# Cross attention on one core: head 3 scaled on VectorE, and V's last low-weight rows as a pair of 64-row matmuls

## The chip, the cores and the metric

One core of a Trainium2 chip. The metric is the device time of one execution in microseconds, the median of several.

## The reference

For each of 8 sequences, x is 256 x 256 and the context 256 x 192, all fp32; 16 heads of 64:

```python
h = layernorm(x) * gamma + beta
Q = (h @ Wq).reshape(B, 256, 16, 64)
K = (context @ Wk).reshape(B, 256, 16, 64)
V = (context @ Wv).reshape(B, 256, 16, 64)
attn = softmax(einsum("bihd,bjhd->bhij", Q, K)) * 64 ** -0.5
vals = einsum("bhij,bjhd->bihd", attn, V).reshape(B, 256, 1024)
out = x + vals @ Wo + bo
```

The scale stands behind the softmax, so no part of it can be moved into Q.

## The kernel before, in words

Products are made in fp32r, and each operand is split into a high part (the rounded value) and a low part (what the rounding left). A product is then high x high, high x low and low x high. ScalarE makes the high parts, VectorE or GpSimd the low parts. Scores are of these products; the probabilities and V stay whole.

The work is cut into 32 steps of four heads (two pairs a = 0, 1), four steps for a sequence. Each engine has its own list, written out by hand in a function `step(u)`, and runs through it in order; semaphores tie the lists together. TensorE's step u is: scores of step u; the first products of the next step's K (`keys_rest`); V x P of step u - 1 (`mix`); K and Q for step u + 1 (`keys`, `queries`); the output product of step u - 1 (`output`); in some steps the transposes of the next context (u = 4, 8, ...) or of the next x (u = 5, 9, ...); V (`values(u + 1)`, each a quarter of a sequence's V); and the transposes of step u's probabilities (`turn`), a first half for heads 0 and 1 and a second for heads 2 and 3. A step without a context or an x to turn is called ordinary below.

The softmax of step u: VectorE takes the maximum of each head's scores (`maximum`, L647), ScalarE the exponentials and their sums (`probabilities`, L457), VectorE the reciprocal of the sums (`inverse`, L654), and GpSimd scales the four heads, two instructions each (L369). ScalarE and VectorE copy the transposed probabilities out of PSUM (L541, L737). Between the heads the lists hold the high and low parts of the mix (L484, L696) and of the next K and Q (`keys_hi`, L467, and `keys_lo`, L660), which also free two PSUM banks: `values` writes its first half where the first pair's K and Q were, its second half where the second's were, and waits for `qk_lo_ready` each time.

V: the context has 192 columns, held as three K tiles of `c_t`: tile 0 the high part of the first 128, tile 2 their low part, and tile 1 both parts of the last 64, low part in the lower 64 partitions and high part in the upper. The weights' last 64 rows stand twice in tile 1 of `wv_hi` and `wv_lo`. `c_rest` holds the high part of the last 64 once more in the lower partitions; before the change only `keys_rest` uses it, for a pair of 64-row matmuls on the two row halves.

x: two buffers. SyncE loads sequence b into the buffer of b - 2 once GpSimd has normalised x (`x_norm`) and added the output bias to it (`x_bias`, L339). VectorE takes its statistics (`statistics`: two bn_stats L582, two bn_aggr L587, L590), GpSimd the power -0.5 (`deviation`, L324) and the normalisation (`norm`, L332; sequences 0 and 1 on VectorE, L596). For sequence b from 2 on the statistics belong to step 4b - 5. Weights arrive in 25 pieces; their low parts are made by VectorE (pieces 0, 4, 5, 8, 9, 13, 20, 21) or GpSimd (L318) in the first steps.

Of the kernel before, what the change touches and what calls it, by code (L numbers as in the profile page):

```python
# [6 lines left out]
def cross_attention_block(nc, x, ctx_in, w_q, w_k, w_v, w_o, b_o, gamma, beta, out):  # L7
# [10 lines left out]
    P = 128  # L18
# [49 lines left out]
    with ExitStack() as ctx:  # L68
# [60 lines left out]
        def qk_banks(u):  # L129

            return ring[u % 3]
# [60 lines left out]
        scaled = sem("scaled")  # L192
# [110 lines left out]
        def _(pool):  # L303
# [51 lines left out]
            def step(u, turns):  # L355
                if u == 1:
                    weight_lo(14)
                b = 1 if u == 1 else of_seq(u, TURN_C, 2)
                if b is not None:
                    deviation(b)  # L360
                    if b >= 2:
                        norm(b)
                if u == PER_SEQ:
                    weight_lo(23)
                if 0 <= u < STEPS:
                    for e in range(HEADS):
                        pool.wait_ge(inv_ready, HEADS * u + e + 1)
                        for r in range(RT):
                            last = nc.gpsimd.tensor_scalar(prob[:, e, r, :], prob[:, e, r, :],  # L369
                                                           inv[:, e, r:r + 1], SCALE,  # L370
                                                           ALU.mult, ALU.mult)
                        last.then_inc(scaled, 1)
                        if e == 1 and u == 2:
                            weight_lo(19)
                for n in {0: (10, 11, 12), 1: (15, 16, 17, 18)}.get(u, ()):
                    weight_lo(n)
                b = of_seq(u, SPLIT_H, 1)
                if b is not None:
                    hidden_lo(b)
                if u == 2:  # L380
                    weight_lo(22)

                    pool.wait_ge(bo_in, 16)
                    bias(0)

                b = 1 if u == PER_SEQ else b if u > PER_SEQ else None
                if b is not None:
                    if b >= 2:

                        pool.wait_ge(y_ready, b - 1)  # L390

                    pool.wait_ge(x_norm_ready, b + 1)
                    bias(b)
# [5 lines left out]
        def _(act):  # L399
# [42 lines left out]
            def step(u):  # L442
# [48 lines left out]
                if u == 2:  # L491
                    weight_hi(20)
                    weight_hi(21)
                    keys_hi(1)
                probabilities(3)
                if u != 2:
                    keys_hi(1)
# [69 lines left out]
        def _(dve):  # L567
# [10 lines left out]
            def statistics(b):  # L578
                k = b % 2
                dve.wait_ge(x_loaded[k], 16 * (b // 2 + 1))  # L580
                for r in range(RT):
                    last = nc.vector.bn_stats(bn[:, r, :], x_in[:, k, r, :])  # L582
                last.then_inc(stats_done, 1)
                dve.wait_ge(stats_done, b + 1)
                nc.vector.memset(var_eps[:, :], 0.0)
                for r in range(RT):
                    last = nc.vector.bn_aggr(mean_var[:, r, :], bn[:, r, :])  # L587
                last.then_inc(aggr_done, 1)
                dve.wait_ge(aggr_done, b + 1)
                nc.vector.tensor_scalar(var_eps[:, :], mean_var[:, :, 1], EPS, None, ALU.add)\  # L590
                    .then_inc(var_ready, 1)

# [34 lines left out]
            def step(u):  # L627
# [27 lines left out]

                def keys_lo(a):
# [17 lines left out]
                inverse(1)  # L674
                b = of_seq(u, PUT)
# [26 lines left out]
                if u == -1:  # L702
                    weight_lo(4)
                keys_lo(0)
                if u == -1:
                    weight_lo(5)
                if u != 2:
                    inverse(3)
# [6 lines left out]
                if u == 0:  # L715
                    statistics(1)
                if u == 1:
                    norm(1)
# [4 lines left out]
                if u == 2:  # L723
                    inverse(3)
# [3 lines left out]
                b = of_seq(u, STATS, 2)  # L728
                if b is not None:
                    statistics(b)  # L730
                if 0 <= u < STEPS:
# [8 lines left out]
                    if u == 0:  # L740
                        weight_lo(13)
# [5 lines left out]
        def _(pe):  # L747
# [189 lines left out]
            def turn(u):  # L937

                for a in range(BATCH):
                    pe.wait_ge(scaled, HEADS * u + 2 * a + 2)  # L940
# [9 lines left out]
            def values(n):  # L950


                g, j = divmod(n, RT)
# [6 lines left out]
                for a, ps in enumerate(((mix_ps, o_ps, mix_ps)[n],) if n <= RT else qk_banks(n)):  # L960
                    columns = PIECE if n <= RT else V_HALF
                    if n > RT:

                        pe.wait_ge(qk_lo_ready, BATCH * n + a + 1)
                    for m, (w, i, k) in enumerate(passes):
                        if m == CT and j == 0 and g in FOR_V:
                            low_ready(pe, FOR_V[g])
                        last = nc.tensor.matmul(ps[:, 0:columns], c_t[:, b % 2, k, rows],  # L968
                                                w[:, i, first:first + columns],
                                                start=m == 0, stop=m == len(passes) - 1,  # L970
                                                skip_group_check=True)
                    first += columns
# [81 lines left out]
```

## Time and profile before

| | |
|---|---|
| median of 3 runs | 335.07 us (335.03 to 335.29) |
| the profiled execution | 335.13 us, its span 333.3 |
| TensorE matmul | 323.3 us, 97% of the span |
| ScalarE | 254.8 us, 76% |
| VectorE | 234.6 us, 70% |
| GpSimd | 178.3 us, 53% |
| granted TensorE clock | full in all 40 slices |

Matmuls overlap in the records: one of 256 columns is recorded with 0.28 us, though the next starts 0.11 behind it. So TensorE's busy share says that it always has something in flight, not how much of its peak it reaches; the distance between starts is what counts. Times in the text are microseconds from the start of the span.

### The profile page before, as it was taken

Reading aid. Unit: us, or ns where it says so; the run is one execution under the profiler, and the core shown is the slowest. Engines: PE = TensorE matmul, PEld = TensorE weight load, DVE = VectorE, ACT = ScalarE, POOL = GpSimd, SP = SyncE. Lnnn points to the kernel's source line nnn. Section 1 sums busy time; section 2 is a strip of 40 time slices with the busy share of each in tenths; the row PEclk is TensorE's granted clock in tenths of the full one; section 3 lists DMA queues with packets and bytes.
Section 4 is the critical chain, followed back from the end, with each engine's and each line's share of the span. In section 5 each row is a group of like instructions: output and inputs, shape, how many; then the busy total and the mean of one; then the engine's idle time right before and its main releaser. Section 6 shows DMA issues by size and latency. Waiting matters only on the chain.

```text
span 333.3 us, 9654 instructions
## 1 busy us (share of the span) xinstructions
PE 323.3 (97%) x3773; PEld 284.3 (85%) x3773; DVE 234.6 (70%) x523; ACT 254.8 (76%) x799; POOL 178.3 (53%) x332
## 2 busy tenths in 40 slices
PE   5999999999999999999999999999999999999986
PEld 4868788899888899888889988889988888998864
DVE  5888667766778677676776677776677867556754
ACT  4899897777778766888667868777777876676772
POOL 4596778437473367543673456722757336344430
PEclk9999999999999999999999999999999999999999
DMA  6960010020000200020000200002000100000000
GB/s 181 266 185 3 1 41 18 2 89 2 0 2 31 60 3 0 2 89 2 3 4 0 89 2 2 0 3 89 2 2 1 33 3 3 2 0 33 2 3 31
DMA packets 10764, 10.70 MB, mean 32 GB/s; under 512 B 960, under 2 KB 10176, under 8 KB 10720
## 3 DMA queue, kind: packets, MB, share of 16 engines
q1 hardware_dynamic: 10192, 9.64, 9.6%
q8 instruction: 30, 0.49, 0.6%
q10 hardware_dynamic: 416, 0.33, 0.3%
q0 software_dynamic: 112, 0.13, 0.1%
q14 instruction: 14, 0.11, 0.1%
HBM read 8.00 MB, written 2.10 MB: 30 GB/s over the span
## 4 chain that ended last, share of the span: by engine, by line
PE 86%; ACT 6%; DVE 4%; POOL 2%; DMA 1%; issue 1%; DVEq 0%; ACTq 0%
PE mix_ps L823 16%; PE o_ps L914 12%; PE ring_ps L794 12%; PE ring_ps L889 12%; PE ring_ps L968 11%; PE ring_ps L944 10%; PE ring_ps L847 9%; ACT prob L457 3%; DMA x_in<-in_x_dram 1%; PE ring_ps L867 1%; POOL prob L369 1%; PE mix_ps L760 1%; PE mix_ps L768 1%; ACT qk_hi L467 1%; DVE prob_t L737 1%
## 5 line engine op out<-in xcount | busy, mean ns | idle before, releaser
L369 POOL TENSOR_SCALAR prob<-prob,inv 128x256 f32<-128x256 f32 x256 | 120.4, 486 | 129.2 <-DVE inv L654 129.1
L457 ACT ACTIVATE prob<-ring_ps,neg_max 128x256 f32<-128x256 f32 x256 | 119.3, 481 | 21.7 <-DVE neg_max L647 21.6
L647 DVE TENSOR_REDUCE neg_max<-ring_ps 128x2 f32<-128x512 f32 x128 | 81.4, 679 | 0.8 <-PE ring_ps L794 0.8
L737 DVE COPY prob_t<-ring_ps 128x512 f32<-128x512 f32 x64 | 41.4, 686 | 37.0 <-PE ring_ps L944 37.0
L823 PE MATMUL mix_ps<-prob_t,v_sb 128*64 128x256 f32 x504 | 61.5, 385 | 0.2 <-DVE prob_t L737 0.2
L660 DVE TENSOR_TENSOR qk_lo<-ring_ps,qk_hi 128x512 fp32r<-128x512 f32 x64 | 44.2, 690 | 17.7 <-ACT qk_hi L467 17.7
L457 ACT ACTIVATION_READ_ACCUMULATOR prob<-ring_ps,neg_max 128x1 f32 x256 | 54.4, 212 | 0.0
L823 PEld LDWEIGHTS mix_ps<-prob_t,v_sb 128*64 128x64 f32 x504 | 33.4, 136 | 18.1 <-issue 0.3
L527 ACT ACTIVATE v_sb<-ring_ps 128x256 f32<-128x256 f32 x58 | 19.2, 383 | 30.1 <-PE ring_ps L968 29.6
L467 ACT ACTIVATE qk_hi<-ring_ps 128x512 fp32r<-128x512 f32 x64 | 39.6, 619 | 1.2 <-PE ring_ps L889 1.2
L944 PE MATMUL ring_ps<-ident,prob 64*128 64x64 f32 x1024 | 39.3, 226 | 0.3 <-POOL prob L369 0.3
L794 PE MATMUL ring_ps<-qk_hi 64*128 64x256 f32 x256 | 39.1, 301 | 0.4 <-DVE qk_lo L660 0.3
L944 PEld LDWEIGHTS ring_ps<-ident,prob 64*128 64x128 f32 x1024 | 34.5, 139 | 5.1 <-POOL prob L369 1.0
L541 ACT ACTIVATE prob_t<-ring_ps 128x512 f32<-128x512 f32 x64 | 35.2, 599 | 3.3 <-PE ring_ps L944 2.1
L847 PEld LDWEIGHTS ring_ps<-c_t,w_hi 128*128 128x128 f32 x192 | 26.4, 188 | 11.9 <-issue 11.5
L794 PE MATMUL ring_ps<-qk_lo,qk_hi 64*128 64x256 f32 x256 | 36.1, 277 | 0.0
L914 PE MATMUL o_ps<-wo_hi,mix_hi 128*128 128x256 f32 x124 | 34.5, 278 | 1.7 <-DVE mix_lo L696 1.4
L794 PE MATMUL ring_ps<-qk_hi,qk_lo 64*128 64x256 f32 x256 | 36.1, 277 | 0.0
L847 PE MATMUL ring_ps<-c_t,w_hi 128*128 128x256 f32 x192 | 35.4, 294 | 0.1
L914 PE MATMUL o_ps<-wo_lo,mix_hi 128*128 128x256 f32 x124 | 34.4, 277 | 0.0
L914 PE MATMUL o_ps<-wo_hi,mix_lo 128*128 128x256 f32 x124 | 34.3, 276 | 0.0
L654 DVE RECIPROCAL inv<-sums 128x2 f32<-128x2 f32 x128 | 21.0, 164 | 17.9 <-ACT prob L457 16.6
(110 smaller groups left out, 638.2 us busy)
## 6 DMA issues: line engine op xcount, KB each, us to landing
x_in<-in_x_dram SPq DMA_DIRECT2D x8, 256.0 KB, 2.9
out_dram<-y_sb SPq DMA_DIRECT2D x7, 256.0 KB, 2.2
c_in<-in_ctx_dram SPq DMA_DIRECT2D x7, 192.0 KB, 2.8
w_raw<-in_L_xattn_Wq_dram SPq DMA_DIRECT2D x8, 128.0 KB, 3.1
w_raw<-in_L_xattn_Wo_dram SPq DMA_DIRECT2D x4, 256.0 KB, 4.0
w_raw<-in_L_xattn_Wk_dram SPq DMA_DIRECT2D x4, 128.0 KB, 3.7
w_raw<-in_L_xattn_Wk_dram SPq DMA_DIRECT2D x8, 64.0 KB, 3.5
w_raw<-in_L_xattn_Wv_dram SPq DMA_DIRECT2D x2, 256.0 KB, 4.7
```

The costliest lines, as they stand in the source:

```text
L369: last = nc.gpsimd.tensor_scalar(prob[:, e, r, :], prob[:, e, r, :], inv[:, e, r:r + 1], SCALE, ALU.mult, ALU.mult)
L457: last = nc.scalar.activation(prob[:, e, r, :], score_bank(u, e)[:, r * ROWS:(r + 1) * ROWS], ACT.Exp, bias=neg_max[:, e, r:r + 1], accum_ ...
L467: nc.scalar.activation(qk_hi[:, a, :, 0:ROWS], qk_banks(u + 1)[a][:, :].rearrange("p (a b) -> p a b", b=ROWS), ACT.Copy)\
L647: nc.vector.tensor_reduce(neg_max[:, e, :], score_bank(u, e)[:, :].rearrange("p (r j) -> p r j", r=RT), AX, ALU.max, negate=True).then_inc ...
L660: nc.vector.tensor_tensor(qk_lo[:, a, :, 0:ROWS], qk_banks(u + 1)[a][:, :] .rearrange("p (a b) -> p a b", b=ROWS), qk_hi[:, a, :, 0:ROWS]. ...
L737: nc.vector.tensor_copy(turned_half(e), score_bank(u, e)[:, :] .rearrange("p (k i) -> p k i", i=HALF))\
L794: last = nc.tensor.matmul(score_bank(u, 2 * a + h)[:, r * ROWS:(r + 1) * ROWS], q[own, a, 1, r * P:(r + 1) * P], key[own, a, 0, 0:ROWS], s ...
L823: last = nc.tensor.matmul(ps[h * HALF:(h + 1) * HALF, first:first + ROWS], v_sb[:, w // RT % 2, j, p * P + h * HALF:p * P + (h + 1) * HALF ...
L847: nc.tensor.matmul(ps[:, 0:ROWS], w[:, i, cols], c_t[:, b % 2, k, :], start=not shared and w is w_hi and i == K0 and k == 0, stop=w is pas ...
L889: last = nc.tensor.matmul(ps[:, ROWS:2 * ROWS], w[:, Q0 + d, cols], h[:, b % 2, d, :], start=n == 0 and d == 0, stop=n == 2 and d == DT - ...
L914: last = nc.tensor.matmul(o_ps[:, r * D:(r + 1) * D], m[:, a, r * P:(r + 1) * P], wt[:, o, cols], start=s == 0 and a == 0 and n == 0 and r ...
L944: last = nc.tensor.transpose(score_bank(u, 2 * a + half)[:, k * HALF:(k + 1) * HALF], prob[own, 2 * a + h, r, j * P:(j + 1) * P], ident[ow ...
```

## The change

It has four parts. VectorE scales head 3 (`last_head`), in steps 0 and 1 behind K and Q's first low part, from step 2 on behind the second; GpSimd keeps heads 0 to 2, and the semaphore `scaled` becomes two. ScalarE makes K and Q's second high part ahead of head 3's exponentials from step 2 on (before: in step 2 alone). The statistics of x are spread over VectorE's step, those of sequence 1 go to the end of step 0, and GpSimd normalises sequence 1. From step 2's second V block on, each half of V has four whole-array matmuls instead of five, and a pair of 64-row matmuls at the end of the block replaces the two that are left out; the pair takes the weights' low part of the last 64 rows with the high part of the context alone (its low part was multiplied too).

```diff
@@ gpsimd step @@
                     deviation(b)
-                    if b >= 2:
-                        norm(b)
+                    norm(b)
...
-                    for e in range(HEADS):
+
+                    for e in range(HEADS - 1):
                         pool.wait_ge(inv_ready, HEADS * u + e + 1)
...
-                        last.then_inc(scaled, 1)
+                        last.then_inc(scaled_pool, 1)
@@ scalar step @@
+                if u >= 2:
                     keys_hi(1)
                 probabilities(3)
-                if u != 2:
+                if u < 2:
                     keys_hi(1)
@@ vector @@
+            def rows_statistics(b, r):
                 k = b % 2
                 dve.wait_ge(x_loaded[k], 16 * (b // 2 + 1))
+                nc.vector.bn_stats(bn[:, r, :], x_in[:, k, r, :]).then_inc(stats_done, 1)
+
+            def variance(b):
+                dve.wait_ge(stats_done, RT * (b + 1))
                 nc.vector.memset(var_eps[:, :], 0.0)
                 for r in range(RT):
                     last = nc.vector.bn_aggr(mean_var[:, r, :], bn[:, r, :])
                 last.then_inc(aggr_done, 1)
+
+            def deviation_base(b):
                 dve.wait_ge(aggr_done, b + 1)
                 nc.vector.tensor_scalar(var_eps[:, :], mean_var[:, :, 1], EPS, None, ALU.add)\
                     .then_inc(var_ready, 1)
...
+                def last_head():
+
+                    inverse(HEADS - 1)
+                    if 0 <= u < STEPS:
+                        dve.wait_ge(inv_ready, HEADS * u + HEADS)
+                        for r in range(RT):
+                            last = nc.vector.tensor_scalar(prob[:, HEADS - 1, r, :],
+                                                           prob[:, HEADS - 1, r, :],
+                                                           inv[:, HEADS - 1, r:r + 1], SCALE,
+                                                           ALU.mult, ALU.mult)
+                        last.then_inc(scaled_vector, 1)
...
                 inverse(1)
+
+                measured = of_seq(u, STATS, 2)
+                if measured is not None:
+                    rows_statistics(measured, 0)
                 b = of_seq(u, PUT)
...
                 inverse(2)
                 if u == -1:
                     weight_lo(4)
+                if measured is not None:
+                    rows_statistics(measured, 1)
                 keys_lo(0)
+                if measured is not None:
+                    variance(measured)
                 if u == -1:
                     weight_lo(5)
-                if u != 2:
-                    inverse(3)
+                if u < 2:
+                    last_head()
...
-                if u == 0:
-                    statistics(1)
-                if u == 1:
-                    norm(1)
                 if u == 2:
                     weight_lo(20)
                     weight_lo(21)
                 keys_lo(1)
-                if u == 2:
-                    inverse(3)
+                if measured is not None:
+                    deviation_base(measured)
+                if u >= 2:
+                    last_head()
                 b = of_seq(u, TURN_C, 2)
                 if b is not None:
                     context_lo(b, context_bank(b))
-                b = of_seq(u, STATS, 2)
-                if b is not None:
-                    statistics(b)
...
                     if u == 0:
+                        statistics(1)
                         weight_lo(13)
@@ tensor @@
-                    pe.wait_ge(scaled, HEADS * u + 2 * a + 2)
+                    pe.wait_ge(scaled_pool, (HEADS - 1) * u + 2 + a)
+                    if a == BATCH - 1:
+                        pe.wait_ge(scaled_vector, u + 1)
...
+                for a, ps in enumerate(qk_banks(n)):
+
+                    pe.wait_ge(qk_lo_ready, BATCH * n + a + 1)
+                    for m, (w, i, k) in enumerate(passes[:-1]):
                         if m == CT and j == 0 and g in FOR_V:
                             low_ready(pe, FOR_V[g])
+                        nc.tensor.matmul(ps[:, 0:V_HALF], c_t[:, b % 2, k, rows],
+                                         w[:, i, first + a * V_HALF:first + (a + 1) * V_HALF],
+                                         start=m == 0, stop=False, skip_group_check=True)
+                pe.wait_ge(c_rest_ready, b + 1)
+                high = (c_rest[:, b % 2, rows], c_t[HALF:P, b % 2, 1, rows])
+                for a, ps in enumerate(qk_banks(n)):
+                    own = slice(a * HALF, (a + 1) * HALF)
+                    last = nc.tensor.matmul(ps[:, 0:V_HALF], high[a],
+                                            wv_lo[own, 1, first + a * V_HALF:first + (a + 1) * V_HALF],
+                                            start=False, stop=True, skip_group_check=True)
                 last.then_inc(v_made, 1)
```

## Rows read from the trace of the kernel before

**Rows 1.** The page: the chain that ended last, share of the span by engine
```profile
PE 86%; ACT 6%; DVE 4%; POOL 2%; DMA 1%; issue 1%; DVEq 0%; ACTq 0%
```

**Rows 2.** Who waited for whom, TensorE: us in total, times, longest
```profile
PE o_ps L914 <- DVE mix_lo L696: 1.4, 1, 1.4
```

**Rows 3.** An ordinary step in order of time, TensorE: start us, us, work
```profile
158.89 0.52 PE L968 MATMUL ring_ps<-wv_hi,c_t 128*128 128x256 f32 x3
...
159.49 0.59 PE L968 MATMUL ring_ps<-wv_hi,c_t 128*128 128x256 f32 x3
159.91 0.39 PE L968 MATMUL ring_ps<-wv_lo,c_t 128*128 128x256 f32 x2
160.23 0.28 PE L944 MATMUL ring_ps<-ident,prob 64*128 64x64 f32 x2
```

**Rows 4.** The chain in order of time: start us, us, what
```profile
78.71 1.36 PE o_ps L914 x12
80.07 1.25 PE ring_ps L968 x10
...
99.91 1.18 PE ring_ps L968 x10
```

**Rows 5.** TensorE from 31.2 on; the transposes of one step (ns min/median/max)
```profile
31.21 0.39 PE L794 MATMUL ring_ps<-qk_hi 64*128 64x256 f32 x2
31.44 0.28 PE L794 MATMUL ring_ps<-qk_lo,qk_hi 64*128 64x256 f32 x2
...
L944 PE MATMUL ring_ps<-ident,prob x32: 222/222/273, 150.6 to 151.5; 64*128 64x64 f32 x32
```

**Rows 6.** An ordinary step in order of time, ScalarE and VectorE
```profile
157.15 0.49 ACT L457 ACTIVATE prob<-ring_ps,neg_max 128x256 f32<-128x256 f32 x1
...
157.96 0.23 ACT L457 ACTIVATION_READ_ACCUMULATOR prob<-ring_ps,neg_max 128x1 f32 x1
158.05 0.63 ACT L467 ACTIVATE qk_hi<-ring_ps 128x512 fp32r<-128x512 f32 x1
...
157.31 0.69 DVE L660 TENSOR_TENSOR qk_lo<-ring_ps,qk_hi 128x512 fp32r<-128x512 f32 x1 [0.32 <-ACT qk_hi L467]
...
158.72 0.69 DVE L660 TENSOR_TENSOR qk_lo<-ring_ps,qk_hi 128x512 fp32r<-128x512 f32 x1
161.08 1.29 DVE L737 COPY prob_t<-ring_ps 128x512 f32<-128x512 f32 x2 [1.67 <-PE ring_ps L944]
```

**Rows 7.** Instructions on x_in (ns min/median/max); VectorE in the first ten microseconds
```profile
L596 DVE TENSOR_SCALAR x_norm<-x_in,mean_var,rstd x4: 396/409/576, 6.5 to 29.0; 128x256 f32<-128x256 f32 x4
...
6.49 0.73 DVE L596 TENSOR_SCALAR x_norm<-x_in,mean_var,rstd 128x256 f32<-128x256 f32 x2 [0.62 <-POOL rstd L324]
...
9.11 0.84 DVE L620 TENSOR_TENSOR h_lo<-h_full,h_hi 128x256 fp32r<-128x256 f32 x1
```

**Rows 8.** Step 3: GpSimd, x's load and its landing, VectorE, TensorE
```profile
46.01 1.42 POOL L339 TENSOR_TENSOR x_bias<-x_in,bo_b 128x256 f32<-128x256 f32 x2
...
47.65 0.39 SPq L263 DMA_DIRECT2D x_in<-in_x_dram  x1
...
DMA to landing us min/median/max: 2.7/2.7/2.7
...
47.13 0.69 DVE L696 TENSOR_TENSOR mix_lo<-mix_ps,mix_hi 128x512 fp32r<-128x512 f32 x1 [0.41 <-ACT mix_hi L484]
...
50.54 0.74 DVE L582 BATCH_NORM_STATS2 bn<-x_in 128x6 f32<-128x256 f32 x2
...
48.75 0.28 PE L914 MATMUL o_ps<-wo_hi,mix_hi 128*128 128x256 f32 x1
```

**Rows 9.** Steps 0 and 1: VectorE, GpSimd, TensorE
```profile
22.13 0.76 DVE L574 TENSOR_TENSOR w_lo<-w_raw,w_hi 128x256 fp32r<-128x256 f32 x1 [0.52 <-ACT w_hi L405]
...
25.88 2.75 POOL L369 TENSOR_SCALAR prob<-prob,inv 128x256 f32<-128x256 f32 x6 [1.17 <-DVE inv L654]
...
29.99 0.71 PE L944 MATMUL ring_ps<-ident,prob 64*128 64x64 f32 x16 [0.30 <-POOL prob L369]
```

More of the change, by code:

```diff
@@ L191, in cross_attention_block @@
         inv_ready = sem("inv_ready")
-        scaled = sem("scaled")
+        scaled_pool = sem("scaled_pool")
+        scaled_vector = sem("scaled_vector")
         turned = sem("turned")
@@ L576, in weight_lo @@
                     .then_inc(w_lo_ready, 1)
-            def statistics(b):
+            def rows_statistics(b, r):
                 k = b % 2
                 dve.wait_ge(x_loaded[k], 16 * (b // 2 + 1))
[L581 to L584, printed above, removed]
+                nc.vector.bn_stats(bn[:, r, :], x_in[:, k, r, :]).then_inc(stats_done, 1)
+            def variance(b):
+                dve.wait_ge(stats_done, RT * (b + 1))
                 nc.vector.memset(var_eps[:, :], 0.0)
@@ L591, in statistics @@
                     .then_inc(var_ready, 1)
+            def statistics(b):
+                for r in range(RT):
+                    rows_statistics(b, r)
+                variance(b)
+                deviation_base(b)
             def norm(b):
@@ L654, in inverse @@
                         nc.vector.reciprocal(inv[:, e, :], sums[:, e, :]).then_inc(inv_ready, 1)
+                def last_head():
+                    inverse(HEADS - 1)
+                    if 0 <= u < STEPS:
+                        dve.wait_ge(inv_ready, HEADS * u + HEADS)
+                        for r in range(RT):
+                            last = nc.vector.tensor_scalar(prob[:, HEADS - 1, r, :],
[3 more added lines that the diff above has]
+                        last.then_inc(scaled_vector, 1)
                 def keys_lo(a):
@@ L959, in values @@
                 first = half * PIECE
[L960 to L964, printed above, removed]
+                if n <= RT:
                     for m, (w, i, k) in enumerate(passes):
+                        if m == CT and j == 0:
+                            low_ready(pe, FOR_V[g])
+                        last = nc.tensor.matmul((mix_ps, o_ps, mix_ps)[n][:, :], c_t[:, b % 2, k, rows],
+                                                w[:, i, first:first + PIECE],
+                                                start=m == 0, stop=m == len(passes) - 1,
+                                                skip_group_check=True)
+                    last.then_inc(v_made, 1)
+                    return
+                for a, ps in enumerate(qk_banks(n)):
+                    pe.wait_ge(qk_lo_ready, BATCH * n + a + 1)
+                    for m, (w, i, k) in enumerate(passes[:-1]):
                         if m == CT and j == 0 and g in FOR_V:
                             low_ready(pe, FOR_V[g])
[L968 to L972, printed above, removed]
+                        nc.tensor.matmul(ps[:, 0:V_HALF], c_t[:, b % 2, k, rows],
[8 more added lines that the diff above has]
+                                            start=False, stop=True, skip_group_check=True)
                 last.then_inc(v_made, 1)
```

## The prediction

> **What bounds the kernel now.** I read the profile in this order: busy shares and the chain that ended last, then who waits for whom, then one ordinary step in order of time on TensorE, ScalarE, VectorE and GpSimd, and last the first five steps, where things differ. TensorE holds 86% of the chain that ended last [rows 1]. The longest wait of its matmuls behind the first constants is a single one of 1.4 us, for the low part of the mix in the last step; the others are 0.4 and less [rows 2]. So in the 28 steps between, time is lost or won only where TensorE's own list of work gets shorter or longer, or where a new wait reaches it.
>
> A step is about 9.7 us. A full matmul of 256 columns takes a slot of 0.113 us: twelve output matmuls take 1.36 us of the chain [rows 4]. V's block begins at 158.89 and the first transpose at 160.23, so 1.34 us for ten matmuls where ten slots are 1.13 [rows 3]. Two things make the difference of 0.21. One is that V's second half waits for K and Q's second low part: it ends at 158.72 + 0.69 = 159.41 and the second half starts at 159.49, its first three matmuls lasting 0.59 where the first three last 0.52. In the chain V's block takes 1.25 in ordinary steps and 1.18 in steps that turn a context or an x first [rows 4], so this wait costs 0.07 to 0.08. The other is the change from whole-array matmuls to ones that use 64 rows: the last V matmul starts at 159.91 + 0.39 - 0.28 = 160.02 and the transposes' first weight load only 0.21 later, a slot and some 0.10 in which no load runs ahead.
>
> **The change, part by part.**
>
> *V's pair.* Ten slots become eight and a pair. The number of changes of array shape stays one: it moves from behind V to ahead of the pair. A pair of 64-row matmuls right behind such a change is in the trace: after x is turned, the pair starts at 31.21 and the next at 31.44, so 0.23, as its weights aren't loaded ahead, against 0.12 for a pair in the run of scores [rows 5]. Transposes behind the change pay less for that: their first matmul lasts 0.27 where the usual is 0.22, so 0.05. Counting from the start of the eighth V matmul: before, two more slots (0.226), the change (0.21), 0.05, in all 0.49 until transposes stream; after, the change (0.21) and the pair (0.23), in all 0.44, with the transposes' weights loaded behind the pair. That saves 0.05, not a whole slot. It happens in 28 steps (2, and 4 to 30; step 3 is counted below): 1.4 us. Bounds: 0, if the pair costs all that it saves, and 0.113 x 28 = 3.2, if its weights load unseen. I take 1.4, as rows 5 show the same two shapes in the same order.
>
> The Trainium skill, TensorEngine Tiling (Array Packing), section Key Properties, says that a change of tiling mode drains the engine, while tiles in one mode work in parallel; this trace agrees with both (0.10 lost at the change, 0.12 for a pair). By the rule alone, with one drain before and one after, the sum would be a whole slot a step, 3.2 us; rows 5 put it lower.
>
> *ScalarE's order.* From step 2 on, K and Q's second high part goes ahead of head 3's exponentials. Today these start at 157.15, end at 158.19, and the high part runs from 158.05 to 158.68 [rows 6]. Its input ends at 157.31 + 0.39 = 157.70, so it will start at 157.73 and end at 158.33; VectorE's low part then ends at 158.37 + 0.69 = 159.06 instead of 159.41. V's second half is due at 158.89 + 4 x 0.113 = 159.34, so its wait goes: 0.08 in 15 ordinary steps (4 to 30 without the twelve that turn c or x), 1.2 us. If a quarter of a microsecond elsewhere ate that margin, 0.
>
> *Head 3 on VectorE.* ScalarE's exponentials of head 3 start 0.48 behind the high part's start, at 158.21, and end 1.04 later, 159.25. VectorE's reciprocal ends at 159.45. The trace has no scaling on VectorE; the nearest row is its normalisation of x, the same operation on the same shape: its four lasted 0.40 to 0.58 each, and two in a row took 0.73 [rows 7]. So the head is scaled at 159.49 + 0.73 = 160.22. The transposes of heads 2 and 3 are due some 0.5 behind the first transposes at 160.14, so at 160.62: margin 0.40, cost 0. VectorE is idle for 1.67 before its copy of the turned probabilities at 161.08, which covers the 0.73. GpSimd gives up 0.93 a step, and nothing waits for it there. The copy of V on ScalarE (0.66 from the end of V's block at 160.30) must end before the next scores at some 161.08: it ends at 161.0, tight but in time. In the last step head 3 is no longer queued behind head 2, but V x P waits there for VectorE's first copy and not for the transposes of the second pair, so 0.
>
> *Statistics of x, spread.* From sequence 2 on, the first half of x's statistics goes between the second reciprocal and the low part of the mix, the second between the third reciprocal and K and Q's first low part. Where x is there, VectorE idles 0.4 and 0.32 at these places [rows 6, 8], and one statistics instruction is 0.41, the first 0.33 of it before the next can start: cost 0. But in step 3 x isn't there. Its buffer comes free when GpSimd's bias of sequence 0 ends, at 46.01 + 1.42 = 47.43; the load is issued at 47.65 and lands 2.7 later, 50.35. Today the statistics run at 50.54, unhindered. After the change VectorE asks for x at 46.73 and stands for 3.6 us, and the low part of the mix, at 47.13 today, is queued behind. It would start at 50.37 + 0.33 = 50.70 and end at 51.39; TensorE's output product needs it and starts at 51.43, not 48.75: 2.7 us [rows 8]. Behind it VectorE does reciprocal 2, the other statistics, the first low part, the variances and the second low part, ending near 53.3, just when V's second half is due (51.43 + 0.11 + 1.37 + 0.45), so no second wait. What releases GpSimd's bias (the weights' high part on ScalarE behind step 2's transposes) is not moved. Cost: 2.7, from 2.4 to 3.0.
>
> *The start.* In step 0 the statistics of sequence 1 (18.49 to 19.74) move behind the copies of turned probabilities and ahead of a weight's low part at 22.13, on which the first maximum of step 1 and all of ScalarE's step hang. The copies will end near 21.45, the statistics near 22.6, the weight near 23.2: the maximum starts some 0.4 later than 22.81. In step 1 normalising sequence 1 moves to GpSimd, 2.4 us for two (1.22 each) from about 24.9, so heads 0 to 2 (2.75) end near 30.0 instead of 28.6, and head 3 on VectorE near 30.1. The second transposes of step 1 started at 29.99 [rows 9]. So 0.15 later, from -0.2 (step 0's transposes no longer wait for head 3 on GpSimd) to +0.5.
>
> **Sum.** The profiled execution took 335.13 us (span 333.3, 1.8 around it), as good as the median of 335.07. 335.13 - 1.4 - 1.2 + 2.7 + 0.15 = 335.4.
>
> **Rivals.**
>
> *A whole slot is won (faster).* The pair's weights load during the drain, so the pair costs 0.12 and not 0.23. For it: in rows 5 the loads of the pair behind it do overlap. Against: all changes of shape in the trace show the late load. 335.13 - 3.2 - 1.2 + 2.7 + 0.15 = 333.6. Chance 0.2.
>
> *The wait for x isn't paid (faster).* If TensorE had other work ready. But the output product stands ahead of V and the transposes in its queue. 332.7; chance 0.06.
>
> *VectorE's scaling comes late (slower).* In step 6 and every fourth one after it (six steps) GpSimd makes h's low part and the bias, both with two inputs, while VectorE scales. The largest of the four normalisations was 0.58, beside GpSimd; a VectorE subtraction of the same shape took 0.84 beside GpSimd [rows 7] and its neighbour 0.41. It decides from a duration of some 0.6 each: at 0.84 (0.76 from start to start) head 3 ends at 161.1, 0.5 late, in six steps 2.8 us: 338.2. At half of that 336.8. Chance 0.14.
>
> The Trainium skill, GPSIMD Engine Reference, section Specifications, says that the two engines share SBUF interfaces and collide when VectorE runs in a two-port mode or reads two inputs; rows 7 agree in kind (0.84 against 0.41).
>
> *The pair gives nothing (slower).* Drain, late load and pair cost as much as two full slots: 335.13 - 1.2 + 2.7 + 0.15 = 336.8. Chance 0.1.
>
> *The start slips a microsecond (slower).* The 0.4 of the late maximum and GpSimd's 2.4 add up rather than overlap; ScalarE is busy without a gap through steps 0 and 1, so nothing takes it back: 336.3. Chance 0.08.
>
> **How the numbers follow.** The forecast has 0.42, and its own range, from the bounds of the stall (0.3), the start (0.35) and the second half's wait, is 334.5 to 336.2. A change under 0.2% (334.4 to 335.7) can't be told from none. Faster holds the first two rivals and a little of the forecast's edge, 0.3; slower the last three and that part of the forecast's range above 335.7, 0.33; the same 0.37. The range of 8 in 10 reaches to 333.5 below and 336.9 above and leaves out the wait that isn't paid and the worst of the late scaling.
>
> **What would show it.** In the profile after: statistics on VectorE waiting for a DMA for 3.6 us in step 3, and TensorE's output product behind it waiting 2.7; an ordinary step shorter by 0.13 (9.56 instead of 9.69) and one that turns c or x by 0.05; V's eight matmuls and pair followed by transposes with no gap; no idle time of TensorE before the transposes of heads 2 and 3. It would be wrong if ordinary steps came out near 9.50 (the rival of the whole slot), if TensorE waited for VectorE's scaling in every fourth step, or if the load of x were issued earlier than 47.

## The result, and the profile after

The changed kernel took 339.14 us (337.84 to 340.89, six runs), the kernel before 335.3 us (335.03 to 335.54) beside it: a ratio of 1.0114, 95% interval 1.0082 to 1.0145. It is slower by 3.8 us where 335.4 was predicted and the range ended at 336.9. The kernel before spread over 0.5 us, this one over 3. The profiled execution is the slowest of the six, 340.89 us with a span of 339.1.

The page of the kernel after, the granted clock in 40 slices and the chain by engine [rows 1]:

```profile
PEclk9999995999999999999999999999999999999999
...
PE 78%; ACT 8%; DVE 7%; POOL 3%; DMA 2%; issue 1%; DVEq 0%; SPq 0%; POOLq 0%; ACTq 0%
```

One slice, 51 to 59 us, stands near half. TensorE's share of the chain fell from 86% to 78%. Who TensorE's matmuls waited for [rows 2]:

```profile
PE o_ps L940 <- DVE mix_lo L722: 4.1, 2, 2.7
```

The columns are us in all, times, and the longest: a second wait for the low part of the mix, 2.7 us long, is new. Step 3 in order of time, GpSimd, SyncE, VectorE and TensorE [rows 8]:

```profile
46.74 1.42 POOL L340 TENSOR_TENSOR x_bias<-x_in,bo_b 128x256 f32<-128x256 f32 x2
...
48.39 0.39 SPq L264 DMA_DIRECT2D x_in<-in_x_dram  x1
...
47.29 0.17 DVE L664 RECIPROCAL inv<-sums 128x2 f32<-128x2 f32 x1 [0.16 <-ACT prob L458]
51.22 0.43 DVE L583 BATCH_NORM_STATS2 bn<-x_in 128x6 f32<-128x256 f32 x1 [3.77 <-DMA x_in<-in_x_dram]
51.56 0.67 DVE L722 TENSOR_TENSOR mix_lo<-mix_ps,mix_hi 128x512 fp32r<-128x512 f32 x1
...
52.38 0.55 PE L940 MATMUL o_ps<-wo_hi,mix_hi 128*128 128x256 f32 x1 [2.71 <-DVE mix_lo L722]
52.73 0.41 PE L940 MATMUL o_ps<-wo_hi,mix_lo 128*128 128x256 f32 x1
52.95 0.41 PE L940 MATMUL o_ps<-wo_lo,mix_hi 128*128 128x256 f32 x1
```

VectorE stands 3.77 us for x, and TensorE 2.71 behind it (forecast: 3.6 and 2.7). What was not forecast is in the last two rows: matmuls that start 0.22 apart instead of 0.11 and last 0.41 instead of 0.28. The busy times by stretch show the clock. The columns are the length, busy time and count of PE, PEld, DVE, ACT and POOL, the granted clock, the DMA share and GB/s:

```profile
50.00:52.40 2.40, 0.02 (x1) 0.05 (x1) 1.18 (x4) 1.21 (x5) 0.00 (x0) 0.85 0.45 149
52.40:55.00 2.60, 2.60 (x12) 2.60 (x13) 2.32 (x10) 0.00 (x0) 1.65 (x3) 0.50 0.00 0
55.00:58.70 3.70, 3.70 (x42) 3.48 (x42) 0.21 (x1) 0.91 (x3) 2.42 (x2) 0.52 0.02 7
58.70:68.00 9.30, 9.30 (x100) 8.23 (x98) 7.12 (x16) 7.62 (x24) 5.44 (x9) 1.00 0.01 2
```

The granted clock is 0.85 on average over the idle stretch, so it fell before TensorE had work again; behind it TensorE works at 0.50, 1.2 instead of 2.4 GHz, until some 58.7. The same in the chain in order of time, where twelve output matmuls take 2.90 at one time and 1.36 at another [rows 4]:

```profile
48.39 2.81 DMA x_in<-in_x_dram
52.38 2.90 PE o_ps L940 x12
...
95.05 1.36 PE o_ps L940 x12
96.41 0.94 PE ring_ps L1005 x8
97.67 0.99 PE ring_ps L972 x32
```

An ordinary step [rows 3]:

```profile
135.68 0.52 PE L1005 MATMUL ring_ps<-wv_hi,c_t 128*128 128x256 f32 x3
136.03 0.28 PE L1005 MATMUL ring_ps<-wv_lo,c_t 128*128 128x256 f32 x1
136.15 0.52 PE L1005 MATMUL ring_ps<-wv_hi,c_t 128*128 128x256 f32 x3
136.50 0.28 PE L1005 MATMUL ring_ps<-wv_lo,c_t 128*128 128x256 f32 x1
136.72 0.38 PE L1012 MATMUL ring_ps<-wv_lo,c_rest 64*128 64x256 f32 x1
...
136.94 1.15 PE L972 MATMUL ring_ps<-ident,prob 64*128 64x64 f32 x32
```

The pair starts 0.22 behind the eighth matmul and the transposes 0.22 behind the pair; V's second half no longer waits (0.52 and not 0.59). In a step where GpSimd makes h's low part, VectorE, GpSimd and TensorE:

```profile
126.15 0.17 DVE L664 RECIPROCAL inv<-sums 128x2 f32<-128x2 f32 x1 [0.22 <-ACT prob L458]
126.35 1.34 DVE L672 TENSOR_SCALAR prob<-prob,inv 128x256 f32<-128x256 f32 x2
127.82 1.46 DVE L762 COPY prob_t<-ring_ps 128x512 f32<-128x512 f32 x2
...
125.36 1.43 POOL L352 TENSOR_TENSOR h_lo<-h_full,h_hi 128x256 fp32r<-128x256 f32 x2 [0.48 <-DVE h_hi L743]
126.76 1.51 POOL L340 TENSOR_TENSOR x_bias<-x_in,bo_b 128x256 f32<-128x256 f32 x2
...
127.03 1.52 PE L972 MATMUL ring_ps<-ident,prob 64*128 64x64 f32 x32
```

Two scalings take 1.34, and the transposes last 1.52 instead of 1.15, as their second half waits. Two of the prediction's own signs are read here: "no idle time of TensorE before the transposes of heads 2 and 3" did not come, and the one against it, "if TensorE waited for VectorE's scaling in every fourth step", did. Step 2, VectorE, GpSimd and TensorE:

```profile
38.78 1.83 DVE L576 TENSOR_TENSOR wv_lo<-w_raw,wv_hi 128x512 fp32r<-128x512 f32 x2
...
38.95 2.26 POOL L352 TENSOR_TENSOR h_lo<-h_full,h_hi 128x256 fp32r<-128x256 f32 x2 [0.43 <-DVE h_hi L743]
...
40.67 0.73 PE L993 MATMUL mix_ps<-wv_lo,c_t 128*128 128x512 f32 x2 [0.49 <-DVE wv_lo L576]
```

**By steps.** From each profile I took the start of the first V x P matmul of every step; the length of step u is the distance to that of step u + 1. "h" are steps 6, 10, ... 26, the ones in which GpSimd makes h's low part; "turning" are those that turn a c or an x from step 8 on; the last three columns are medians.

```
                         step 1   2      3      4      ordinary turning  h
before                    9.81  11.56   9.69  10.05    9.69    10.06    9.69
after                    10.28  12.06  15.24  10.13    9.54     9.99    9.90
a (statistics 2 late)    10.28  12.03   9.80  10.13    9.54     9.99    9.90
b (bias first)           10.28  12.06   9.56   9.99    9.55     9.99    9.90
c (behind the mix)       10.28  12.05  13.24  10.00    9.55     9.99    9.90
k (before, with wait)     9.76  11.53  12.57  10.05    9.69    10.06    9.69
d (pair alone)            9.76  11.51   9.73  10.13    9.74     9.99    9.73
n (order alone)           9.75  11.58   9.62  10.08    9.63    10.06    9.61
e (pair and order)        9.77  11.48   9.67   9.98    9.54     9.99    9.54
f (a, head 3 on GpSimd)  11.03  11.51   9.54  10.13    9.66    10.13    9.67
g (a, GpSimd waits)      10.28  12.03   9.80  10.13    9.54     9.99    9.54
h (a, start as before)    9.41  11.54   9.81  10.13    9.54     9.99    9.90
m (change mended)         9.37  11.58   9.55  10.13    9.67    10.13    9.66
p (e once more)           9.75  11.52   9.55  10.13    9.67    10.13    9.66
```

So the 5.8 us between the two profiled spans are, to 0.1: +0.7 up to step 3, +5.55 in step 3, +0.2 in steps 4 and 5 (whose whole-array matmuls stand 0.118 apart instead of 0.113, see the last section), six times +0.21 in the h steps, eight times -0.15 in ordinary steps, -0.14 in step 30, and ten times -0.07 in turning ones.

### The profile page after: what moved, and what is told of

It is laid out like the page before. It is cut to its first block, busy times and chain, and to the rows that moved or that the text cites. A ratio compares the mean times of both kernels' runs of the same rounds, so it can differ in the third digit from the quotient of the medians.

```text
span 339.1 us, 9687 instructions
## 1 busy us (share of the span) xinstructions
PE 324.7 (96%) x3773; PEld 285.1 (84%) x3773; DVE 258.3 (76%) x585; ACT 254.6 (75%) x799; POOL 152.0 (45%) x270
## 4 chain that ended last, share of the span: by engine, by line
PE 78%; ACT 8%; DVE 7%; POOL 3%; DMA 2%; issue 1%; DVEq 0%; SPq 0%; POOLq 0%; ACTq 0%
PE mix_ps L849 15%; PE ring_ps L820 12%; PE ring_ps L915 11%; PE o_ps L940 10%; PE ring_ps L873 9%; PE ring_ps L972 8%; PE ring_ps L1005 7%; ACT prob L458 4%; PE ring_ps L1012 2%; DVE prob L672 2%; DMA x_in<-in_x_dram 2%; ACT qk_hi L468 2%; PE ring_ps L893 1%; POOL prob L370 1%; POOL wo_lo L319 1%
## 5 line engine op out<-in xcount | busy, mean ns | idle before, releaser
L370 POOL TENSOR_SCALAR prob<-prob,inv 128x256 f32<-128x256 f32 x192 | 89.7, 484 | 151.1 <-DVE inv L664 151.0
L458 ACT ACTIVATE prob<-ring_ps,neg_max 128x256 f32<-128x256 f32 x256 | 118.0, 473 | 21.7 <-DVE neg_max L657 21.6
L458 ACT ACTIVATION_READ_ACCUMULATOR prob<-ring_ps,neg_max 128x1 f32 x256 | 52.7, 206 | 0.0
L468 ACT ACTIVATE qk_hi<-ring_ps 128x512 fp32r<-128x512 f32 x64 | 38.8, 606 | 14.3 <-PE ring_ps L915 14.3
L820 PE MATMUL ring_ps<-qk_hi 64*128 64x256 f32 x256 | 39.8, 301 | 0.3 <-DVE qk_lo L682 0.3
L940 PE MATMUL o_ps<-wo_hi,mix_hi 128*128 128x256 f32 x124 | 35.3, 284 | 4.4 <-DVE mix_lo L722 4.1
L972 PEld LDWEIGHTS ring_ps<-ident,prob 64*128 64x128 f32 x1024 | 36.7, 140 | 2.9 <-POOL prob L370 1.4
L543 ACT ACTIVATE prob_t<-ring_ps 128x512 f32<-128x512 f32 x64 | 36.0, 606 | 3.4 <-PE ring_ps L972 3.4
L820 PE MATMUL ring_ps<-qk_hi,qk_lo 64*128 64x256 f32 x256 | 36.9, 277 | 0.0
L820 PE MATMUL ring_ps<-qk_lo,qk_hi 64*128 64x256 f32 x256 | 36.8, 277 | 0.0
```

The source lines that it names most:

```text
L458: last = nc.scalar.activation(prob[:, e, r, :], score_bank(u, e)[:, r * ROWS:(r + 1) * ROWS], ACT.Exp, bias=neg_max[:, e, r:r + 1], accum_ ...
L468: nc.scalar.activation(qk_hi[:, a, :, 0:ROWS], qk_banks(u + 1)[a][:, :].rearrange("p (a b) -> p a b", b=ROWS), ACT.Copy)\
L820: last = nc.tensor.matmul(score_bank(u, 2 * a + h)[:, r * ROWS:(r + 1) * ROWS], q[own, a, 1, r * P:(r + 1) * P], key[own, a, 0, 0:ROWS], s ...
L940: last = nc.tensor.matmul(o_ps[:, r * D:(r + 1) * D], m[:, a, r * P:(r + 1) * P], wt[:, o, cols], start=s == 0 and a == 0 and n == 0 and r ...
L972: last = nc.tensor.transpose(score_bank(u, 2 * a + half)[:, k * HALF:(k + 1) * HALF], prob[own, 2 * a + h, r, j * P:(j + 1) * P], ident[ow ...
```

## The experiments

Times are medians; each kernel's ratio is to runs of the kernel before beside it.

### The wait for x

**a**: sequence 2's statistics at the end of step 3.

```diff
-                measured = of_seq(u, STATS, 2)
+                measured = of_seq(u, STATS, 3)
...
+                if u == PER_SEQ - 1:
+                    statistics(2)
```

> The changed kernel, with the statistics of sequence 2 alone put back behind step 3's context_lo, where they stood before the change. Theory 1 (the wait for x in step 3, and the clock that falls behind it, carry the loss): step 3, from its scores to the next scores, took 15.3 us in the profiled run after and 9.75 before; without the wait it takes 9.6, so 340.9 - 5.7 = 335.2, 0.3 less if the slower matmuls of the three steps behind go too: 335.0, with the clock at 1.000 and runs within 0.5 us of each other. Theory 2 (the loss is spread: the start, 0.7, and VectorE's scaling beside GpSimd in six steps, which make up for each other with little else): the time stays above 337. Theory 3 (the wait costs only its own 2.7 and the clock is no part of it): 338.2 where the profiled run was 340.9.

335.53 us (335.23 to 336.4), ratio 1.0007 (0.9998 to 1.0016). The clock is 1.00 throughout, step 3 takes 9.80. Theory 1 holds to 0.5 us: without this one place the change is level with the kernel before. That is not yet the forecast: with the wait's 2.7 taken off, the forecast for such a kernel is 332.7.

**c**: the first statistics one instruction later, behind the low part of the mix.

```diff
-                if measured is not None:
+                if measured is not None and measured != 2:
                     rows_statistics(measured, 0)
...
+                if measured == 2:
+                    rows_statistics(measured, 0)
                 if measured is not None:
                     rows_statistics(measured, 1)
```

> The changed kernel, with sequence 2's first statistics behind the low part of the mix, ahead of K and Q's first low part. x lands at 51.2 as before; the output product no longer waits for it, V does: VectorE makes both statistics by 52.0 and the first low part by 52.6, V is due at 50.9, so TensorE idles 1.7 instead of 2.7. If the clock falls after any such idle time: 340.9 - 1.0 = 339.9 at worst, the spread of the runs stays, and the granted clock in the slice behind is half. If it falls only behind the longer one: 335.0 + 1.7 = 336.7, clock 1.000, a small spread.

337.71 us (336.8 to 338.86), ratio 1.0053 (1.0039 to 1.0067). TensorE waits 1.7, now in V. Its profiled execution was the slowest of its runs, and its stretches (the idle one, and the one behind it):

```profile
51.00:53.20 2.20, 0.51 (x4) 0.31 (x3) 1.62 (x7) 0.48 (x3) 0.15 (x1) 1.00 0.26 86
53.20:56.00 2.80, 2.80 (x26) 2.37 (x25) 1.22 (x5) 0.50 (x2) 1.99 (x3) 0.60 0.03 6
```

The clock falls behind 1.7 us too: step 3 costs 3.7 more than 9.54, 1.7 of wait and 2.0 behind it, where the clock is 0.60. The other four runs, at 336.8 to 337.8, have a mean clock of 0.999 or 1.000, so theirs didn't fall. Neither branch of the expectation was right as put: the clock fell behind the shorter wait in one run of five.

**k**: the kernel before, with only this wait put in: sequence 2's first statistics instruction moves forward.

```diff
-                for r in range(RT):
+                for r in range(1 if b == 2 else 0, RT):
                     last = nc.vector.bn_stats(bn[:, r, :], x_in[:, k, r, :])
...
                 inverse(1)
+                if u == PER_SEQ - 1:
+                    dve.wait_ge(x_loaded[0], 32)
+                    nc.vector.bn_stats(bn[:, 0, :], x_in[:, 0, 0, :])
```

> The kernel before, whole, with one thing moved: sequence 2's first statistics instruction stands in step 3 ahead of the low part of the mix. Theory 1 (the wait for x, with the clock that falls behind it, is enough for the loss): the output product of step 3 starts 2.7 later, a slice of the granted clock shows half, step 3 takes 15 us instead of 9.7, and the time is between 338.3 (clock stays) and 341.2 (clock falls as in the profiled run after), with a wide spread of runs. Theory 2 (the wait is hidden in part, and the loss comes from the rest of the change): under 337.

339.85 us (338.58 to 340.17), ratio 1.0131 (1.0116 to 1.0145): as much as the whole change. The profiled execution is the fastest of the four and shows the same idle time with the clock left alone:

```profile
50.00:52.50 2.50, 0.70 (x6) 0.73 (x7) 1.86 (x6) 0.08 (x1) 0.68 (x2) 1.00 0.27 92
52.50:55.00 2.50, 2.50 (x33) 2.37 (x33) 1.21 (x6) 0.36 (x2) 2.09 (x5) 1.00 0.03 7
```

There step 3 takes 12.57, 2.9 over 9.69, near the forecast's 2.7; the other three runs have a mean clock of 0.995 and take 1.1 to 1.6 us more. So the wait costs its length always, and the clock's fall in some executions: three of these four, three of the changed kernel's six (mean clock 0.995, 0.995 and 0.989; its other three at 1.000), one of c's five. That spreads the runs, but not alone: the changed kernel's three runs at 1.000 stand at 337.84, 337.96 and 338.79.

The Trainium skill, TensorE: Matmul & The Clock Gate, Part 1, says that a monitor in the hardware gates TensorE's clock to half when the engine was little used of late and releases it after sustained work, on a schedule that doesn't start with the kernel. The two levels agree with the 0.50 and 1.00 here; that the schedule is what makes k fall in three runs of four, no run here can show.

**b**: the changed kernel, x loaded earlier.

```diff
                 if u == 2:
-                    weight_lo(22)
-
                     pool.wait_ge(bo_in, 16)
                     bias(0)
+                    weight_lo(22)
```

> The changed kernel whole, with one pair of lines swapped on GpSimd in step 2: the bias of sequence 0 (which frees x's buffer) ahead of weight piece 22's low part, where it no longer waits for ScalarE. GpSimd is free at 41.2, the bias ends at 42.6, x of sequence 2 is issued near 42.8 and lands near 45.6, ahead of 47.5, when VectorE asks for it. Theory 1 (the place of the statistics is harmless, only x's lateness costs): no wait in step 3, clock 1.000, step 3 at 9.54 and not 9.80 as with the statistics at its end, 335.3. Theory 2 (the early statistics hold up the low part of the mix even where x is there): output product late in step 3 and in each statistics step, above 336.

335.49 us (335.14 to 336.07), ratio 1.0011 (1.0002 to 1.0021). VectorE, step 3:

```profile
47.55 0.17 DVE L663 RECIPROCAL inv<-sums 128x2 f32<-128x2 f32 x1 [0.16 <-ACT prob L457]
47.63 0.41 DVE L582 BATCH_NORM_STATS2 bn<-x_in 128x6 f32<-128x256 f32 x1
48.12 0.69 DVE L721 TENSOR_TENSOR mix_lo<-mix_ps,mix_hi 128x512 fp32r<-128x512 f32 x1
```

With x there the early statistics cost nothing that can be told, and step 3 is 9.56. Swapping two pieces of work on GpSimd takes the wait away. What keeps this kernel at the level of the one before is then not x: the forecast without the wait's 2.7 is 332.7.

### V's pair and the order of the second high part

**d**: the kernel before with V's pair alone (the `values` of the change). **n**: with the order alone:

```diff
@@ scalar @@
+                if u >= 2:
                     keys_hi(1)
                 probabilities(3)
-                if u != 2:
+                if u < 2:
                     keys_hi(1)
@@ vector @@
-                if u != 2:
+                if u < 2:
                     inverse(3)
...
                 keys_lo(1)
-                if u == 2:
+                if u >= 2:
                     inverse(3)
```

**e** and **p** are one kernel with both.

> The kernel before, with V's pair and nothing else of the change. Theory 1 (V's second half hangs on K and Q's second low part): in the 16 ordinary steps its start is fixed at 159.49 by that low part, so only one slot (0.113) is dropped behind it and the pair costs 0.23 less the 0.05 that the transposes save: 0.07 more a step; in the 12 steps that turn c or x 0.05 less. Sum +0.5 us: 335.8, no change that can be told. Theory 2 (the pair saves 0.05 wherever it stands): 335.3 - 1.4 = 333.9. Theory 3 (a whole slot each): 332.1.

335.33 us (335.0 to 335.69), ratio 0.999 (0.9981 to 0.9999). Ordinary steps 9.74 where 9.76 was expected, turning ones 9.99. The pair without the order wins 0.1% at most.

> The kernel before, with the order of the second high and low part and of head 3's exponentials and reciprocal alone; V as before. The pair alone left ordinary steps at 9.74 and those that turn c or x at 9.99; both together gave 9.54 and 9.99. Theory 1 (the order takes away V's second wait, 0.08, and nothing else): ordinary 9.61, turning ones 10.05, 335.6 - 15 x 0.08 = 334.4. Theory 2 (the order pays only with the pair): 9.69, 335.6.

334.39 us (334.16 to 334.46), ratio 0.9977 (0.9969 to 0.9986). Ordinary steps 9.63, turning ones unchanged: theory 1.

> The kernel before, with V's pair and with ScalarE's second high part ahead of head 3's exponentials and VectorE's second low part ahead of the fourth reciprocal from step 2 on. Head 3 stays on GpSimd, statistics and normalisation stay where they were. Theory 1: the second half's wait (0.08 in 15 steps) and the pair's 0.05 in 28 steps are won, GpSimd ends head 3 at 160.47 of a step whose transposes are due at 160.62: 335.3 - 1.2 - 1.4 = 332.7, ordinary steps of 9.54, clock 1.000. Theory 2 (head 3 on GpSimd comes late now that its exponentials are later, which is what VectorE's scaling is for): from 0.2 late in 27 steps on the gain is gone, 335 to 338.

332.14 us (331.96 to 332.26), ratio 0.9899 (0.9883 to 0.9914). Every ordinary and h step 9.54, turning ones 9.99. Head 3 on GpSimd is in time, so VectorE's scaling isn't needed for this gain.

> The kernel of e_pair_and_order once more, beside the others on one chip, for more executions. Several of the kernels above took one of two times from run to run (333.3 or 336.6 with the clock at 1.000), with matmuls 0.118 apart in one and 0.113 in the other. If that belongs to short steps as such, some of these runs are near 335; if not, all are at 332.1.

332.26 us, ratio 0.9944 (0.9912 to 0.9976), but four runs at 332.0 to 332.3 and three at 335.4, all at clock 1.00. The chain of e, and of p's profiled run at 335.39, in a step of each that turns a context:

```profile
208.75 1.47 PE ring_ps L795 x24
...
212.87 0.68 PE ring_ps L890 x6
...
214.68 1.37 PE o_ps L915 x12
```

```profile
214.91 0.71 PE ring_ps L890 x6
...
216.79 1.42 PE o_ps L915 x12
...
220.90 1.47 PE ring_ps L795 x24
```

Whole-array matmuls stand 0.113 apart in e (twelve take 1.37) and 0.118 in p's run (1.42); the pairs of the scores take 1.47 in both.

### VectorE's scaling beside GpSimd

**f** is a with head 3 on GpSimd. **g** is a with head 3 on VectorE and one wait more:

```diff
                 if b is not None:
+                    if u > 2:
+                        pool.wait_ge(scaled_vector, u + 1)
                     hidden_lo(b)
```

> The kernel of a_stats2_late with head 3 scaled by GpSimd in every step (VectorE makes the reciprocal only). There the six steps in which GpSimd makes h's low part and the bias (6, 10, ... 26) take 9.90 where ordinary ones take 9.54. Theory 1 (VectorE's scaling collides with them): they come to 9.54, 335.5 - 6 x 0.36 = 333.4. Theory 2 (these steps are long for what VectorE and ScalarE do for h, and head 3's place is indifferent): 335.5. If head 3 on GpSimd is late in ordinary steps, above that.

334.77 us (333.51 to 337.24), ratio 0.9993 (0.9968 to 1.0018). The runs stand in groups: three at 333.5 to 333.8, four at 334.7 to 334.8, all of these at a mean clock of 0.995, and five at 337.0 to 337.2. In its profiled execution (337.24, matmuls 0.118 apart from step 4 on) h steps and ordinary steps are alike, 9.67 and 9.66: theory 1, by the steps and not by the median. Four heads behind the normalisation cost step 1 another 0.75; TensorE idles there for 1.11 at one place.

> The kernel of a_stats2_late with head 3 on VectorE everywhere, but from step 6 on GpSimd starts h's low part only when VectorE's scaling of that step is done. The same instructions on the same engines, only no longer at the same time. Theory 1 (the collision of the two engines lengthens each scaling from 0.35 to 0.82 us): scalings at 0.35 in all steps, 9.54 in steps 6, 10, ..., 333.4. Theory 2 (VectorE's queue is too long in these steps whatever GpSimd does): 9.9 stays, 335.5.

333.39 us, ratio 0.9976 (0.9948 to 1.0004): seven runs at 333.1 to 333.4, five at 336.4 to 336.7. VectorE and GpSimd in an h step of the profiled execution (333.37):

```profile
120.66 0.62 DVE L674 TENSOR_SCALAR prob<-prob,inv 128x256 f32<-128x256 f32 x2
...
121.36 1.42 POOL L352 TENSOR_TENSOR h_lo<-h_full,h_hi 128x256 fp32r<-128x256 f32 x2 [2.17 <-DVE prob L674]
```

The same two scalings take 0.62 and not 1.34, and the step 9.54 and not 9.90. That is the collision by itself: same work, same engines, other time.

### The start, and all of it mended

**h** is a with sequence 1's statistics and normalisation as before the change, and GpSimd's first low part of h behind VectorE's pieces 20 and 21.

> The kernel of a_stats2_late with sequence 1's statistics back in step 0 behind the scaling, its normalisation back on VectorE, and in step 2 GpSimd's first low part of h waiting for VectorE's low parts of pieces 20 and 21. Step 1 took 10.28 (9.81 before the change), step 2 12.03 (11.56). Theory 1 (GpSimd's normalisation holds up heads 0 to 2 in step 1; in step 2 h's low part, no longer behind head 3 on GpSimd, collides with VectorE's low parts of V's weights, 1.83 instead of 1.28): step 1 at 9.8 and step 2 at 11.5, 335.5 - 1.0 = 334.5. Theory 2 (what is lost at the start comes from the scaling on VectorE itself, which stays here): steps 1 and 2 stay at 10.3 and 12.0, 335.5.

336.12 us (334.72 to 337.17), ratio 1.0014 (1.0003 to 1.0025). By its time alone this says theory 2; by its steps theory 1 for step 2: it is 11.54, as it is in f (11.51), where head 3 is back on GpSimd. The first V x P matmul of step 3 starts at 44.65, with a at 45.20, before at 44.50. The three fastest runs are at 334.7 to 335.0, the others above 335.8. Its profiled execution is one of the fast ones, so what holds the others isn't in a profile. For the verdict on the start the steps are what counts: 0.55 us won, of which step 2 is 0.49. Step 1's half of the expectation isn't borne out: that step is 0.87 shorter than in a, but it begins 0.81 later, so that step 2 begins at 33.11, with a at 33.17.

**m** is b with g's wait and h's start.

> The changed kernel with the three places mended: the bias first as in b_bias_first, GpSimd's h low part behind VectorE's scaling as in g_late_gpsimd_waits, and the start as in h_late_start_as_before. From the steps of those runs: steps 6, 10, ... 9.54, step 3 9.54, step 2 11.5, so g's 333.4 - 0.5 - 0.3 = 332.6, level with the pair and the order alone (332.1). If it stays above 334, the three costs don't add up as read.

335.89 us (332.2 to 337.29), ratio 0.9982 (0.9951 to 1.0013). Three runs at 332.2, one at 333.8, five at 335.7 to 335.9, three at 337.0 to 337.3. The profiled one (335.90) has matmuls 0.118 apart from step 4 on, and the step lengths of p to 0.01. So the three costs add up as read, to 332.2, in the three runs of that time. In the profiled one the wider spacing of the matmuls hides it; the runs above and between have no profile, and what holds the three at 337 isn't shown.

## Why the prediction was wrong

**V's pair, ScalarE's order: right, to two hundredths.** Forecast 9.56 for ordinary steps and 0.05 less for turning ones; measured 9.54 and 0.07. The pair saves 0.07 where V's second half isn't waiting and loses 0.05 where it is (d), the order alone gives 0.06 to 0.08 (n), both 0.15 (e). A whole slot, the first rival, is not won.

**Head 3 on VectorE: "margin 0.40, cost 0" is the step that failed.** Uncontended the scaling took 0.35 where 0.40 was taken, and in ordinary steps it is in time. In the six h steps the scalings took up to 0.82 beside GpSimd, and the steps 0.36 more than ordinary ones, 2.2 us in all, in the profile of each kernel that has it (the changed one, a, b, c, h). f (the scaling on GpSimd) and g (on VectorE, at another time) both take the difference away. The rival had this mechanism, 0.5 a step at 0.84; I gave it 0.14 although rows 7 held the 0.84. The miss is there without any wait for x: b was measured at 335.49 where the forecast less the wait's 2.7 is 332.7, and e, which has the pair and the order without the rest of the change, at 332.14.

**The wait for x: its length right, its price short in some runs.** TensorE idled 2.71, for the reason given. Where the clock stayed, that was also the price: the changed kernel's fastest run is 2.7 over b's (337.84 against 335.14), and k's run at 1.000 is 3.0 over the kernel before. In the profiled run, the slowest, it cost 5.55: the matmuls behind it ran at half clock for some six microseconds. "Cost: 2.7, from 2.4 to 3.0" has no term for that; from b's median to the changed kernel's it is 3.6. a, b and k show both sides: without the wait the change is level with the kernel before, and the wait alone makes the kernel before as slow as the changed one. The rows ahead of the prediction held nothing of this, since the kernel before never idles its TensorE for longer than 1.4 us behind the start; that should have widened the term's bound upwards, and it didn't.

**The start: 0.15 forecast, 0.7 between the two profiles, 0.5 of it shown.** The 0.5 is in step 2 and was not seen: with head 3 gone from GpSimd, its low part of h starts 2.5 us earlier, on top of VectorE's low parts of V's weights, which take 1.83 instead of 1.28; V waits for them. In h they stay apart, and step 2 is back. The other 0.2, ahead of step 2, can't be told from the spread: profiles of kernels that are the same up to there begin step 2 at 32.94 and 33.15 (before and k) or at 33.18 and 33.44 (the changed kernel and b).

**The sum.** With the clock left alone the forecast would have been 335.4 + 0.6 (start) + 2.2 (scaling) less some 0.5 for gains a little above the forecast, 337.7; the changed kernel's two fastest runs are 337.84 and 337.96, already outside the range that ended at 336.9. The rest of the median, 1.3 us, is the clock in part: the two runs at 0.995 stand at 339.5 and 339.6. The one at 338.79 has a mean clock of 1.000, and what holds it isn't in a profile.

## What to carry to other kernels

When an instruction with a new wait is moved forward in a queue, look for its first use, not its usual one: in five of six sequences x was there long before, and the one where it wasn't cost as much as the pair and the order had won. On a TensorE that never idles, price an idle stretch as itself, and widen the range upwards for the clock behind it: here by up to as much again behind 2.7 us, and in some runs only. Work that moves to another engine has to be priced beside what runs there and next to it at that time: the slowest row of the nearest kind (0.84 here), not the usual one. And work taken off one engine moves what stood behind it: ask what the earlier start now runs beside, on the other elementwise engine too.

## What the runs showed of the hardware

Whole-array matmuls of 256 columns, each with weights of its own, keep 0.113 or 0.118 us between starts, at a granted clock of 1.00 in both; pairs of 64-row matmuls, transposes and V x P keep theirs (1.47, 0.99 and 1.88 us in the chain of a step, in e and in p's run alike). A step is 9.54 or 9.67. The wider spacing lasts from step 4 to the end (p, m, f) or for stretches of steps (b; steps 4 and 5 of the changed kernel), and one kernel takes 332.2 or 335.4 by it. The pair isn't needed for it: the kernel before has 0.118 in step 1, and k, which has no pair and no short steps, has it in steps 8, 16 and 24 of its profile, which take 10.19 where its other turning steps take 10.05. But the runs of the kernel before and of n, without the pair, lie within 1 us, while those of f, g, h, m and p, with the pair and short steps, lie over 2.4 to 5.1 us. What chooses between the two stays open: no experiment here separates the causes. It also means that the gain of e is 1.0% at one spacing and none at the other.

The clock. Four kernels have a stretch of more than 1 us between the start and the last steps in which TensorE idles: 2.71 us in the changed kernel, 2.61 in k, 1.69 in c, 1.11 in f. Of their 27 runs 11 have a mean granted clock of 0.995 or less, 4 of them f's. The nine others (a, b, d, e, g, h, m, n, p) idle for 0.6 at most in their profiles, and none of their 90 runs is below 0.999. Where the clock fell in f isn't in a profile, as its profiled execution is at 1.00.

Two changes of tile shape cost as forecast: the pair starts 0.22 behind the whole-array matmul and the transposes 0.22 behind the pair, where matmuls of one shape stand 0.11 apart.
